# Perceiver layer on one core: heads stage reordered two groups ahead, and the row maxima of W1 taken in the cross-attention

## The chip, the cores and the metric

The kernel runs on one core of a Trainium2 chip (trn2). The metric is the device time of one execution in microseconds. Engines: PE is TensorE, DVE VectorE, ACT ScalarE, POOL GpSimd; SP issues most of the DMAs.

## The reference, cut to what matters

```python
def layer(x, ctx):                       # x [1, 256, 1024], ctx [1, 4096, 1024], all float32
    y = layernorm(x)                     # cross-attention
    Q, K = y @ Wq.T + bq, ctx @ Wk.T + bk
    x = x + softmax(Q @ K.T / sqrt(1024)) @ ctx
    y = layernorm(x)                     # latent attention, 128 heads, 8 content and 64 rope dims each
    cq, ckv = y @ Wq_down, y @ Wkv_down
    q_c, k_c, v_c = heads(cq @ Wq_up), heads(ckv @ Wk_up), heads(ckv @ Wv_up)
    q_r, k_r = heads(y @ Wq_rope), y @ Wk_rope          # k_r is shared by all heads
    s = (q_c @ k_c.T + q_r @ k_r.T) / sqrt(72)
    x = x + merge(softmax(s) @ v_c) @ Wo
    y = layernorm(x)                     # two quantized linears, 1024 -> 4096 -> 1024
    # linear8(x, W, b): columns of x whose maximum is over 3 stay whole; all else is rounded to
    # int8 codes, with a scale per row of x and a scale per row of W: max |W[n, :]| / 127
    return x + linear8(linear8(y, W1, b1), W2, b2)
```

## The kernel before, in words

Every product of float32 values is made of three float32r matmuls: each operand is split into a high part (a cast copy) and a low part (the value less its high part), and `product` (lines 45 to 51) issues high x high, high x low and low x high. ScalarE mostly makes the high parts, VectorE and GpSimd the low ones. Engines meet at semaphores, and each engine runs its own list in order. The stages follow each other in blocks, and an engine starts a block when all have ended the one before.

**Scores** (about 82 to 195 us). ctx comes in eight chunks of 512 rows, 2 MB each, into two `ring` buffers. TensorE turns a chunk while it multiplies the chunk before. Per chunk VectorE makes eight low parts, two score maxima, and the row maxima of two W2 panels: a panel is 128 rows x 1024 columns, 512 KB, loaded into `w2p` (`load_w2` L420, `maximum_w2` L425).

**Attend** (about 195 to 298 us). The chunks are loaded again. For each chunk ScalarE makes the exponentials, the high part of the chunk's rows (`high_rows`, L407) and the high part of the turned probabilities. VectorE and GpSimd make the low parts of two row tiles each (`low_rows`, L412), VectorE those of the probabilities (`low_p`, L675), and then VectorE takes two more W2 panels. TensorE works on chunk c while the parts of c + 1 are made. SP's list for a chunk: two panels, a wait for the low parts of the chunk (n_dve, n_pool), the load of the chunk after next. When all is done VectorE divides and adds for each of two row tiles (L701) and makes the layernorm.

**Projections** (302 to 329 us). Down and up projections; the content parts of q and k go to DRAM (`store_content`), in three slots of 128 rows, so that a group can read them back in another layout. VectorE copies the low and the high part of k_r to eight head slots each (L905, L906).

**Heads** (330 to 731 us). 128 heads in 32 groups of four. A group's rope weights (128 x 8 x 256, 1 MB) are loaded to `ring`, split by ScalarE (two `wh` copies, L774) and GpSimd (two subtractions, L780), and multiplied: `rope_q`, 48 matmuls, one PSUM bank for each pair of heads. ScalarE copies each head's q to `qrope` (L1117) and again to rows 0 to 63 of `qmix` (L1118); VectorE puts the low part on the other half of `qrope` (L1178). Rows 64 to 87 of `qmix`, `kmix_h` and `kmix_l` hold the content slots, read by GpSimd's three DMAs (L1232). `scores_q` (2 matmuls a head) gives rough scores from which VectorE takes negated maxima (L1187), `turn_max` turns them, ScalarE copies a row for each head to row 96 of `qmix` (L1143); `scores_k` (4 matmuls a head) gives key-major scores with the maximum subtracted; ScalarE makes exp (L1124) and its high part (L1128), VectorE the low part (L1183); `attend` (4 matmuls a head) multiplies with the values that GpSimd has put in place (L1240). VectorE also takes one W1 row tile's maxima per group (L1199). Per group TensorE has 48 + 8 + 2 + 16 + 16 = 90 matmuls. TensorE's order in a group is written out by hand in `step`: the scores of group g, the attend of g - 1 and the rope products of g + 1. In the last group ScalarE and VectorE also split three pairs of oT tiles (L947, L952) before the rest of their work.

After the heads come the output projection and the two linears (731 to 1061 us), which the change leaves as they are.

## Time and profile before

| | us |
|---|---|
| median of 3 runs | 1061.13 |
| lowest, highest | 1061.06, 1067.21 |
| profiled execution: span | 1060.9 |
| busy: PE, DVE, ACT, POOL | 962.6, 760.3, 697.2, 451.8 |

No time of the profiled execution is given apart from its span. A row of groups gives line, engine, operation, output <- inputs, count, then busy time, the mean of one in ns, and the idle time before with its releaser. Times in the timeline are us from the span's start. A matmul's duration in the profile is longer than its distance to the next, since they are pipelined.

### The profile page before, as it was taken

The page shows a single profiled execution, that of the slowest core. Times are in us where ns is not written, and L with a number is a line of the kernel's source. Part 1 is how long each engine was busy: PE and PEld are TensorE (multiplying, and loading weights), DVE is VectorE, ACT ScalarE, POOL GpSimd, SP SyncE. Part 2 cuts the span into 40 slices and gives each one's busy share as a digit, 9 for nine tenths or more (in the row PEclk, how much of TensorE's full clock was granted, in tenths as well). Part 3 has the DMA queues.
Part 4 walks back from the last instruction along what each step waited for, and adds up shares of the span by engine and source line. Part 5 has one row for each costly group of instructions (what it writes and reads, how often), then busy time and mean ns, then how long its engine had stood idle before and what let it go on. Part 6 is the DMA issues. An engine that isn't in the chain of part 4 may idle for free. (4 is left out here: it accounts for less than half of the span.)

```text
span 1060.9 us, 20413 instructions
## 1 busy us (share of the span) xinstructions
PE 962.6 (91%) x6771; PEld 881.5 (83%) x6771; DVE 760.3 (72%) x1212; ACT 697.2 (66%) x1270; POOL 451.8 (43%) x395
## 2 busy tenths in 40 slices
PE   6999999899978889999999999997859999599987
PEld 5998888688867888998999999986658999498986
DVE  6426566544474678888787889878797888798864
ACT  4424434545345788998999999995538777456562
POOL 0300000433335445655566556630147666355663
PEclk9999999999989899999999999996969999699999
DMA  7436665567625766455545554560424334223221
GB/s 278 160 120 219 237 212 202 215 254 274 201 89 159 204 201 200 156 172 152 154 141 166 175 152 142 174 226 1 159 79 153 111 134 158 80 80 144 95 80 40
DMA packets 71706, 168.36 MB, mean 159 GB/s; under 512 B 7504, under 2 KB 48496, under 8 KB 69104
## 3 DMA queue, kind: packets, MB, share of 16 engines
q1 hardware_dynamic: 66576, 158.35, 43.5%
q0 software_dynamic: 4608, 9.45, 3.6%
q8 instruction: 24, 0.39, 0.1%
q14 instruction: 18, 0.15, 0.0%
q10 hardware_dynamic: 480, 0.03, 0.0%
HBM read 160.46 MB, written 7.34 MB: 158 GB/s over the span
## 5 line engine op out<-in xcount | busy, mean ns | idle before, releaser
L780 POOL TENSOR_TENSOR wl<-ring,wh 128x1024 fp32r<-128x1024 f32 x64 | 153.5, 2400 | 109.8 <-ACT wh L774 109.8
L49 PE MATMUL bank<-act_all,W_all 128*128 128x256 f32 (+1 forms) x512 | 158.0, 309 | 10.7 <-POOL W_all L1483 7.9
L49 PE MATMUL bank<-act_all,wh 128*128 128x256 f32 x512 | 148.1, 289 | 2.0 <-PEq L785 2.0
L51 PE MATMUL bank<-act_all,W_all 128*128 128x256 f32 (+1 forms) x512 | 146.0, 285 | 0.0
L50 PE MATMUL bank<-act_all,wh 128*128 128x256 f32 x512 | 145.0, 283 | 0.0
L51 PE MATMUL bank<-act_all,wl 128*128 128x256 f32 x512 | 144.5, 282 | 0.0
L412 POOL TENSOR_TENSOR xa_WT_l<-ring,xa_WT_h 128x1024 fp32r<-128x1024 f32 x16 | 41.4, 2606 | 186.4 <-ACT xa_WT_h L407 186.4
L1483 POOL TENSOR_TENSOR W_all<-rnd,W_all 128x512 fp32r<-128x512 f32 x72 | 92.9, 1303 | 45.1 <-ACT W_all L1408 38.1
L49 PEld LDWEIGHTS bank<-act_all,W_all 128*128 128x128 f32 x512 | 99.8, 195 | 13.4 <-POOL W_all L1483 9.9
L1183 DVE TENSOR_TENSOR pl<-pexp,ph 128x512 fp32r<-128x512 f32 x128 | 85.8, 689 | 25.5 <-ACT ph L1128 25.1
L49 PEld LDWEIGHTS bank<-act_all,wh 128*128 128x128 f32 x512 | 98.9, 193 | 2.8 <-issue 2.8
L51 PEld LDWEIGHTS bank<-act_all,W_all 128*128 128x128 f32 x512 | 99.7, 195 | 0.0
L50 PEld LDWEIGHTS bank<-act_all,wh 128*128 128x128 f32 x512 | 98.4, 192 | 0.0
L51 PEld LDWEIGHTS bank<-act_all,wl 128*128 128x128 f32 x512 | 98.1, 192 | 0.0
L1785 POOL TENSOR_TENSOR W_all<-rnd,W_all 128x512 fp32r<-128x512 f32 x56 | 73.1, 1316 | 54.8 <-ACT W_all L1743 54.0
L1128 ACT ACTIVATE ph<-pexp 128x512 fp32r<-128x512 f32 x128 | 80.9, 632 | 10.6
L1178 DVE TENSOR_TENSOR qrope<-bank,qrope 64x256 fp32r<-64x256 f32 x128 | 54.0, 422 | 45.2 <-ACT qmix L1118 42.0
L1187 DVE TENSOR_REDUCE nmax<-bank 128x2 f32<-128x512 f32 x128 | 82.7, 688 | 3.6 <-PE bank L1017 2.5
L1035 PE MATMUL bank<-qrope,krope 128*128 128x256 f32 x256 | 71.9, 301 | 12.3 <-ACT qmix L1143 7.0
L774 ACT ACTIVATE wh<-ring 128x1024 fp32r<-128x1024 f32 x64 | 67.4, 1056 | 20.1 <-DMA ring<-in_L_attn_Wq_rope_dram 18.3
L1124 ACT ACTIVATE pexp<-bank 128x512 f32<-128x512 f32 x128 | 75.3, 588 | 2.7 <-PE bank L1036 1.2
L50 PE MATMUL bank<-W_all 128*128 128x256 f32 (+1 forms) x256 | 73.9, 289 | 0.0
(221 smaller groups left out, 2885.2 us busy)
## 6 DMA issues: line engine op xcount, KB each, us to landing
ring<-in_ctx_dram SPq DMA_DIRECT2D x16, 2048.0 KB, 8.7
ring<-in_L_attn_Wq_rope_dram SPq DMA_DIRECT2D x32, 1024.0 KB, 7.1
ring<-in_L_ffn_W_dram SPq DMA_DIRECT2D x16, 2048.0 KB, 7.5
w2p<-in_L_ffn_W_dram SPq DMA_DIRECT2D x32, 512.0 KB, 4.7
w1p<-in_L_ffn_W_dram SPq DMA_DIRECT2D x32, 512.0 KB, 3.5
ring<-in_L_xattn_Wq_dram SPq DMA_DIRECT2D x2, 2048.0 KB, 11.8
ring<-in_L_xattn_Wk_dram SPq DMA_DIRECT2D x2, 2048.0 KB, 7.9
ring<-in_L_attn_Wo_dram SPq DMA_DIRECT2D x2, 2048.0 KB, 11.4
```

Source lines behind the costliest of these rows:

```text
L49: pe.matmul(out, lh, rh, start=start, stop=False, skip_group_check=True)
L50: pe.matmul(out, lh, rl, start=False, stop=False, skip_group_check=True)
L51: return pe.matmul(out, ll, rh, start=False, stop=stop, skip_group_check=True)
L774: act.activation(wh[b][:, 4 * half:4 * half + 4, :], rope_raw(b)[:, 4 * half:4 * half + 4, :], ACT.Copy).then_inc(w_hi, 1)
L780: pool.tensor_tensor(wl[b][:, 4 * half:4 * half + 4, :], rope_raw(b)[:, 4 * half:4 * half + 4, :], f32(wh[b][:, 4 * half:4 * half + 4, :]) ...
L1035: pe.matmul(o, krope[:, kt * P:(kt + 1) * P], qrope[b][:, h, :], start=True, stop=False)
L1124: act.activation(pexp[h % 2][:, :, :].rearrange("p k q -> p (k q)"), bank[5 + h % 2][:, :], ACT.Exp, scale=RSQRT).then_inc(ex_ready, 1)
L1128: act.activation(ph[h][:, :, :], pexp[h % 2][:, :, :], ACT.Copy).then_inc(p_hi, 1)
L1183: dve.tensor_tensor(pl[h][:, :, :], pexp[h % 2][:, :, :], f32(ph[h][:, :, :]), ALU.subtract).then_inc(p_lo, 1)
L1187: dve.tensor_reduce(nmax[b][:, :, 32 * h:32 * h + 1], bank[3 + h % 2][:, :].rearrange("p (t k) -> p t k", t=QT), axis=AX.X, op=ALU.max, ne ...
L1483: pool.tensor_tensor(W_l[b][:, k, :], rnd[k % 4][:, :], f32(W_h[b][:, k, :]), ALU.subtract).then_inc(b_lo, 1)
L1785: pool.tensor_tensor(V_l[:, k, :], rnd[k % 4][:, :], f32(V_h[:, k, :]), ALU.subtract).then_inc(j_lo, 1)
```

## The change

**W1 maxima moved.** The panel buffers of scores and attend (now `panel`, still two) take W1 row tiles as well: per chunk of scores two W2 panels and one of W1, per chunk of attend two of W2 and three of W1; all 32 W1 tiles are done there, and the heads take none. SP loads panels 0 and 1 of a chunk ahead of the ctx load and the others behind it. A panel's load waits for the maximum taken from the panel two before it.

**Heads.** TensorE's step g now holds attend(g - 1), scores_k(g), scores_q(g + 1) and rope_q(g + 2), with three buffers for `qmix`, `qrope` and the key tiles. The loops are written out for all groups. ScalarE copies q once, to `qrope`; SP copies it from there to `qmix` by DMA (`duplicate`, two per pair of heads). `kmix` is the one key tile: it holds the low part of k_r (spread by three DMAs instead of sixteen casts), the same content rows for both kinds of scores, and in rows 96 to 99 a one for the own head; `krope` has two forms, one for heads with the high part of q in the lower half and one for the others. The four maxima rows are written by one operation (`max_rows`) to all four heads' rows 96 to 99. The second half of the weights' high part is copied by GpSimd instead of ScalarE. The content is read by SP, two DMAs per group instead of three by GpSimd, and the content stores come behind one another in the first six steps. The three oT copies of ScalarE stand at the start of the last step, VectorE's parts of them at its end.

```diff
-            w2_ready, w2_max = [sem("w2_ready0"), sem("w2_ready1")], sem("w2_max")
-            def load_w2(sp, n, j):
-                sp.wait_ge(w2_max, n * 2 + (j + 1))
-                sp.dma_start(w2p[j][:, :], w2_flat[:, ds(n * (2 * D) + j * D, D)]).then_inc(w2_ready[j], 16)
-            def maximum_w2(dve, n, j):
-                dve.wait_ge(w2_ready[j], n * 16 + 16)
-                dve.tensor_reduce(am2[:, ds(n * 2 + j, 1)], w2p[j][:, :], axis=AX.X, op=ALU.max,
-                                  apply_absolute_value=True).then_inc(w2_max, 1)
+            panel_ready, panel_max = [sem("panel_ready0"), sem("panel_ready1")], sem("panel_max")
+            IN_SCORES, IN_ATTEND = 3, 5
+            def load_panel(sp, q, b, src):
+                sp.wait_ge(panel_max, q + 1)
+                sp.dma_start(panel[b][:, :], src).then_inc(panel_ready[b], 16)
+            def maximum_panel(dve, b, uses, out):
+                dve.wait_ge(panel_ready[b], uses * 16 + 16)
+                dve.tensor_reduce(out, panel[b][:, :], axis=AX.X, op=ALU.max, apply_absolute_value=True).then_inc(panel_max, 1)
+            def w1_rows(n):
+                return w1_n[ds(n, 1)].rearrange("a p d -> p (a d)")
...
+            def attend_panels(i, b):
+                at = IN_ATTEND * b
+                return [(i * 10 + (NCTX * IN_SCORES + at + p), (at + p) % 2, i * 5 + (NCTX * IN_SCORES // 2 + (at + p) // 2))
+                        for p in range(IN_ATTEND)]
...
+                            load_panels(i, b, (0, 1))
                             sp.wait_ge(sb_ready, i * (2 * KT) + KT * (b + 1))
                             load(sp, b, raw(b), ctx_t[ds(i * 2 + (b + 2), 1)].rearrange("a p t d -> p (a t) d"))
+                            load_panels(i, b, (2,))
...
+                    def step(i, b, ahead):
+                        c = i * 2 + b
+                        panels = scores_panels(i, b)
+                        outs = (am2[:, ds(c * 2, 1)], am2[:, ds(c * 2 + 1, 1)], am1[:, ds(c, 1)])
                         for k in range(KT):
                             if ahead:
                                 low(1 - b, k, c * KT + (KT + k + 1))
-                            if k % 4 == 1:
-                                maximum_w2(dve, c, k // 4)
+                            if k in (1, 4, 6):
+                                p = (1, 4, 6).index(k)
...
+                        def load_panels(i, b, which):
+                            c = i * 2 + b
+                            sources = [w2_flat[:, ds(c * (2 * D) + (NCTX * 2 + j) * D, D)] for j in range(2)]
+                            sources += [w1_rows(c * 3 + (NCTX + j)) for j in range(3)]
+                            for p in which:
+                                q, buf, _ = attend_panels(i, b)[p]
+                                load_panel(sp, q, buf, sources[p])
                         with sp.Fori(0, NCTX // 2 - 1) as i:
                             for b in range(2):
-                                for j in range(2):
-                                    load_w2(sp, i * 2 + (NCTX + b), j)
+                                load_panels(i, b, (0, 1))
                                 sp.wait_ge(n_dve, i * 4 + 2 * (b + 1))
                                 sp.wait_ge(n_pool, i * 4 + 2 * (b + 1))
                                 load(sp, b, raw(b), ctx_t[ds(i * 2 + (b + 2), 1)].rearrange("a p t d -> p (a t) d"))
+                                load_panels(i, b, (2, 3, 4))
...
+                        def maxima(i, b):
+                            c = i * 2 + b
+                            outs = [am2[:, ds(c * 2 + (NCTX * 2 + j), 1)] for j in range(2)]
+                            outs += [am1[:, ds(c * 3 + (NCTX + j), 1)] for j in range(3)]
+                            for (_, buf, uses), o in zip(attend_panels(i, b), outs):
+                                maximum_panel(dve, buf, uses, o)
+                        def chunk(i, b):
+                            c = i * 2 + b
+                            low_rows(dve, c, b, (0, 1), n_dve)
+                            low_p(c, b)
+                            maxima(i, b)
...
+            QBUF = 3
             vals = sb(ml, "vals", [P, 2, QT, D], F32R)
-            krope = sb(ml, "krope", [P, T], F32R)
-            kmix_l = sb(ml, "kmix_l", [P, 2 * GROUP, T], F32R)
-            kmix_h = sb(ml, "kmix_h", [P, 2 * GROUP, T], F32R)
-            qmix = [sb(ml, f"qmix{i}", [P, GROUP, T], F32R) for i in range(2)]
+            krope = sb(ml, "krope", [P, 2, T], F32R)
+            kmix = sb(ml, "kmix", [P, QBUF * GROUP, T], F32R)
+            qmix = [sb(ml, f"qmix{i}", [P, GROUP, T], F32R) for i in range(QBUF)]
...
-            def split_w(act, b, half):
-                act.activation(wh[b][:, 4 * half:4 * half + 4, :], rope_raw(b)[:, 4 * half:4 * half + 4, :],
-                               ACT.Copy).then_inc(w_hi, 1)
-            def low_w(pool, g2, b):
-                for half in range(2):
-                    pool.wait_ge(w_hi, g2 * 2 + (half + 1))
-                    pool.tensor_tensor(wl[b][:, 4 * half:4 * half + 4, :], rope_raw(b)[:, 4 * half:4 * half + 4, :],
-                                       f32(wh[b][:, 4 * half:4 * half + 4, :]), ALU.subtract).then_inc(w_lo, 1)
+            def half_of(tile, half):
+                return tile[:, 4 * half:4 * half + 4, :]
+            def high_w(act, g):
+                landed(act, g % 2, USE_ROPE + g // 2)
+                act.activation(half_of(wh[g % 2], 0), half_of(rope_raw(g % 2), 0), ACT.Copy).then_inc(w_hi, 1)
+            def split_w(pool, g):
+                landed(pool, g % 2, USE_ROPE + g // 2)
+                h, l, r = wh[g % 2], wl[g % 2], rope_raw(g % 2)
+                pool.tensor_copy(half_of(h, 1), half_of(r, 1)).then_inc(w_hi2, 1)
+                pool.wait_ge(w_hi, g + 1)
+                pool.tensor_tensor(half_of(l, 0), half_of(r, 0), f32(half_of(h, 0)), ALU.subtract).then_inc(w_lo, 1)
+                pool.wait_ge(w_hi2, g + 1)
+                pool.tensor_tensor(half_of(l, 1), half_of(r, 1), f32(half_of(h, 1)), ALU.subtract).then_inc(w_lo, 1)
...
+                    sp.wait_ge(kr_hi, 2)
+                    for b in range(QBUF):
+                        sp.dma_start(f32(kmix[0:ROPE, b * GROUP:(b + 1) * GROUP, :]),
+                                     f32(krope[0:ROPE, 1, :]).unsqueeze(1).to_broadcast([ROPE, GROUP, T])).then_inc(k_spread, 16)
...
+                    def content(g):
+                        b = g % QBUF
+                        if g % 8 == 0:
+                            sp.wait_ge(stored[g // 8], 2 * SLOTS * 16)
+                        if g >= QBUF:
+                            sp.wait_ge(st_ready, (g - QBUF + 1) * GROUP)
+                        own = slice(b * GROUP, (b + 1) * GROUP)
+                        columns = slice((g % 4) * GROUP * T, (g % 4 + 1) * GROUP * T)
+                        for dst, i in ((qmix[b], 0), (kmix[:, own, :], 1)):
+                            src = content_dram[i][g // 4].rearrange("(r h) q -> r (h q)", h=HT)
+                            sp.dma_start(f32(dst[ROPE:ROPE + SLOTS * HEAD, :, :]).rearrange("p h q -> p (h q)"),
+                                         src[:, columns]).then_inc(mix_ready[b], 16)
+                    def duplicate(g, pair):
+                        b = g % QBUF
+                        sp.wait_ge(q_hi, g * GROUP + 2 * pair + 2)
+                        for s in range(2):
+                            h = 2 * pair + s
+                            sp.dma_start(f32(qmix[b][0:ROPE, h, :]),
+                                         f32(qrope[b][s * ROPE:(s + 1) * ROPE, h, :])).then_inc(dup_ready[b][pair], 16)
+                    def next_w(g):
+                        sp.wait_ge(w_lo, (g - 1) * 2)
+                        load(sp, g % 2, rope_raw(g % 2), rope_t[:, :, g * GC:(g + 1) * GC])
+                    next_w(2)
+                    for g in range(FIRST, NG):
+                        if valid(g + 2):
+                            content(g + 2)
+                            duplicate(g + 2, 0)
+                        if 0 <= g + 2 < 6:
+                            store_content(sp, 1 + (g + 2) // 2, (g + 2) % 2)
+                        if valid(g + 2):
+                            duplicate(g + 2, 1)
+                        if valid(g + 5):
+                            next_w(g + 5)
+                        elif g + 5 < NG + 2:
+                            b = (g + 5) % 2
+                            sp.wait_ge(w_lo, (g + 4) * 2)
+                            load(sp, b, raw(b), wo_t[:, CH * b:CH * b + CH, :])
...
+                    for g in range(FIRST, NG + 1):
+                        scores_q(g + 1, 0)
+                        attend(g - 1, 0)
+                        attend(g - 1, 1)
+                        rope_q(g + 2, 0, 0)
+                        scores_k(g, 0)
+                        rope_q(g + 2, 0, 2)
+                        attend(g - 1, 2)
+                        scores_q(g + 1, 1)
+                        rope_q(g + 2, 0, 4)
+                        attend(g - 1, 3)
+                        scores_k(g, 1)
+                        rope_q(g + 2, 0, 6)
+                        scores_q(g + 1, 2)
+                        scores_k(g, 2)
+                        rope_q(g + 2, 1, 0)
+                        scores_q(g + 1, 3)
+                        rope_q(g + 2, 1, 2)
+                        rope_q(g + 2, 1, 4)
+                        rope_q(g + 2, 1, 6)
+                        scores_k(g, 3)
+                        turn_max(g + 1)
 
...
+                    def max_rows(g):
+                        if not valid(g):
+                            return
+                        act.wait_ge(nt_ready, g + 1)
+                        act.activation(qmix[g % QBUF][96:100, :, :],
+                                       bank[2][0:GROUP, 0:T].unsqueeze(1).to_broadcast([GROUP, GROUP, T]), ACT.Copy).then_inc(m_row, 1)
...
+                    for g in range(FIRST, NG):
+                        next_w(g + 3)
                         if g == NG - 1:
                             for kk in range(KT // 2 - 1):
                                 act.wait_ge(o_norm, 4 * kk + 4)
                                 ot_high(act, kk)
-                        step(g, g % 2, USE_ROPE + 1 + g // 2, g < NG - 1, g < NG - 2)
+                        exps(g, 0)
+                        high_p(g, 0)
+                        exps(g, 1)
+                        high_q(g + 2, 0)
+                        high_p(g, 1)
+                        exps(g, 2)
+                        high_p(g, 2)
+                        high_q(g + 2, 1)
+                        max_rows(g + 1)
+                        exps(g, 3)
+                        high_p(g, 3)
...
+                    for g in range(FIRST, NG):
+                        maxima(g + 1, 0)
                         low_p(g, 0)
+                        maxima(g + 1, 1)
+                        low_q(g + 2, 0)
                         low_p(g, 1)
-                    low_q(0, 0, 0)
-                    step(0, 0, None, True, 1)
-                    with dve.Fori(0, NG // 4 - 1) as i:
-                        for j in range(4):
-                            step(i * 4 + (j + 1), (j + 1) % 2, (i * 4 + j, i, j), True, i * 2 + ((j + 1) // 2 + 1))
-                    for j in range(3):
-                        g = NG - 3 + j
+                        maxima(g + 1, 2)
+                        maxima(g + 1, 3)
+                        low_p(g, 2)
+                        if valid(g - 1):
+                            outputs(dve, g - 1)
+                            if (g - 1) % 4 == 3:
+                                divide(dve, (g - 1) // 4)
+                        low_q(g + 2, 1)
...
+                        values(g)
+                        if valid(g + 3):
+                            if g + 3 >= 2:
+                                pool.wait_ge(q_ready, (g + 2) * 2)
+                            split_w(pool, g + 3)
```

## Rows read from the trace of the kernel before

**Rows 1.** The page: busy time of each engine over the span.

```profile
PE 962.6 (91%) x6771; PEld 881.5 (83%) x6771; DVE 760.3 (72%) x1212; ACT 697.2 (66%) x1270; POOL 451.8 (43%) x395
```

**Rows 2.** Windows: length, busy us (count) of PE, PEld, DVE, ACT, POOL; PEclk; DMA share; GB/s.

```profile
125.00:150.00 25.00, 25.00 (x139) 20.73 (x138) 15.79 (x22) 9.66 (x18) 0.00 (x0) 1.00 0.62 220
226.66:238.73 12.07, 12.07 (x58) 9.83 (x57) 5.90 (x6) 6.27 (x10) 5.09 (x2) 1.00 0.68 258
329.90:731.00 401.10, 378.02 (x2880) 353.88 (x2880) 315.47 (x526) 349.78 (x705) 210.28 (x222) 0.97 0.55 166
422.33:705.22 282.89, 276.55 (x2162) 259.41 (x2161) 237.58 (x397) 262.65 (x529) 161.34 (x168) 1.00 0.52 161
694.41:705.22 10.81, 10.81 (x92) 10.64 (x91) 9.18 (x17) 10.31 (x22) 6.79 (x7) 1.00 0.63 231
```

**Rows 3.** Groups by line, 422 to 705 us: count, busy us, mean ns, idle before.

```profile
L780 POOL TENSOR_TENSOR wl<-ring,wh 128x1024 fp32r<-128x1024 f32 x48 | 115.4, 2405 | 75.5 <-ACT wh L774 75.5
...
L1183 DVE TENSOR_TENSOR pl<-pexp,ph 128x512 fp32r<-128x512 f32 x97 | 65.0, 689 | 18.5 <-ACT ph L1128 18.3
L1187 DVE TENSOR_REDUCE nmax<-bank 128x2 f32<-128x512 f32 x96 | 61.9, 688 | 0.9
L1128 ACT ACTIVATE ph<-pexp 128x512 fp32r<-128x512 f32 x97 | 61.4, 633 | 8.2
L1124 ACT ACTIVATE pexp<-bank 128x512 f32<-128x512 f32 x96 | 56.5, 589 | 1.2
...
L774 ACT ACTIVATE wh<-ring 128x1024 fp32r<-128x1024 f32 x48 | 50.7, 1056 | 5.5 <-DMA ring<-in_L_attn_Wq_rope_dram 4.9
...
L1178 DVE TENSOR_TENSOR qrope<-bank,qrope 64x256 fp32r<-64x256 f32 x96 | 40.5, 422 | 22.5 <-ACT qmix L1118 20.0
...
L1143 ACT ACTIVATE qmix<-bank 1x256 fp32r<-1x256 f32 x96 | 35.9, 374 | 2.4
L1117 ACT ACTIVATE qrope<-bank 64x256 fp32r<-64x256 f32 x96 | 35.9, 374 | 1.7
```

**Rows 4.** Timeline of SP in attend: start us, us, DMA issue.

```profile
201.28 1.50 SPq L423 DMA_DIRECT2D w2p<-in_L_ffn_W_dram  x2
...
235.06 0.33 SPq L121 DMA_DIRECT2D ring<-in_ctx_dram  x1
236.15 0.92 SPq L423 DMA_DIRECT2D w2p<-in_L_ffn_W_dram  x2
```

**Rows 5.** The page, DMA issues: KB each, median us from issue to landing.

```profile
ring<-in_L_attn_Wq_rope_dram SPq DMA_DIRECT2D x32, 1024.0 KB, 7.1
...
qmix<-content_q POOLq DMA_DIRECT2D x32, 96.0 KB, 2.5
```

**Rows 6.** Timeline of VectorE in attend, one chunk and the end.

```profile
227.75 2.36 DVE L412 TENSOR_TENSOR xa_WT_l<-ring,xa_WT_h 128x1024 fp32r<-128x1024 f32 x2 [5.21 <-ACT xa_WT_h L407]
...
232.28 2.33 DVE L427 TENSOR_REDUCE am<-w2p 128x1024 f32 x2
...
292.60 1.54 DVE L701 SCALAR_TENSOR_TENSOR xr<-bank,rden,xr 128x512 f32<-128x512 f32 x2 [9.51 <-PE bank L51]
...
298.19 1.54 DVE L701 SCALAR_TENSOR_TENSOR xr<-bank,rden,xr 128x512 f32<-128x512 f32 x2 [0.96 <-PE bank L51]
```

**Rows 7.** Landing of single DMAs issued near 196, 201, 235 and 236 us.

```profile
w2p<-in_L_ffn_W_dram SPq DMA_DIRECT2D x1, 512.0 KB, 3.6
...
w2p<-in_L_ffn_W_dram SPq DMA_DIRECT2D x1, 512.0 KB, 7.3
...
ring<-in_ctx_dram SPq DMA_DIRECT2D x1, 2048.0 KB, 7.9
w2p<-in_L_ffn_W_dram SPq DMA_DIRECT2D x1, 512.0 KB, 8.0
```

**Rows 8.** Windows: TensorE at a lower granted clock early in the heads.

```profile
358.40:365.20 6.80, 5.88 (x27) 5.88 (x28) 1.54 (x3) 6.36 (x14) 5.09 (x4) 0.50 0.96 303
```

**Rows 9.** Timeline of TensorE, the matmul before which it sat idle.

```profile
359.32 0.58 PE L1035 MATMUL bank<-qrope,krope 128*128 128x256 f32 x1 [2.96 <-ACT qmix L1143]
```

More of the change, by code:

```diff
@@ L194, in build @@
             rmax = sb(xs, "rmax", [P, QT])
-            w2p = [sb(xs, f"w2p{i}", [P, D]) for i in range(2)]
+            panel = [sb(xs, f"panel{i}", [P, D]) for i in range(2)]
             nbias = sb(xs, "nbias", [P, QT])
@@ L1034, in scores_k @@
                             o = bank[5 + h % 2][:, kt * T:(kt + 1) * T]
-                            pe.matmul(o, krope[:, kt * P:(kt + 1) * P], qrope[b][:, h, :], start=True, stop=False)
-                            last = pe.matmul(o, kmix_l[0:97, b * GROUP + h, kt * P:(kt + 1) * P], qmix[b][0:97, h, :],
-                                             start=False, stop=True)
+                            keys = slice(kt * P, (kt + 1) * P)
+                            pe.matmul(o, krope[:, h % 2, keys], qrope[b][:, h, :], start=True, stop=False)
@@ L1038, in scores_k, with attend @@
+                            last = pe.matmul(o, kmix[0:100, b * GROUP + h, keys], qmix[b][0:100, h, :], start=False, stop=True)
                         last.then_inc(st_ready, 1)
-                    def attend(g, b, h):
+                    def attend(g, h):
+                        if not valid(g):
+                            return
                         if h == 0:
                             pe.wait_ge(val_ready, g * 2 + 2)
-                            pe.wait_ge(o_done, g + 1)
-                        pe.wait_ge(p_lo, g * GROUP + (2 + h + 1))
+                            if g:
+                                pe.wait_ge(o_done, g)
+                        pe.wait_ge(p_lo, g * GROUP + h + 1)
@@ L1096, in _ @@
-                    pe.wait_ge(w_lo, 2)
-                    for pair in range(2):
-                        for k0 in range(0, KT, 2):
-                            rope_q(0, pair, k0)
-                    first_scores(0, 0, 1)
-                    step(0, 0, 1, None, True)
-                    with pe.Fori(0, NG // 2 - 1) as i:
-                        step(i * 2 + 1, 1, i + 2, i * 2, True)
-                        step(i * 2 + 2, 0, i + 2, i * 2 + 1, True)
-                    step(NG - 1, 1, None, NG - 2, False)
```

405 lines of the change are left out of this document (158 added, 247 removed).

## The prediction

> **What bounds the kernel now.** I read the page first: TensorE is busy for 91% of the span, so a gain must come from TensorE's idle time or its pace [rows 1]. Then I cut the span into stages [rows 2]. In a scores step and an attend step TensorE has no gap (25.00 of 25.00 us, 12.07 of 12.07). The heads stage takes 401.10 us for 2880 matmuls. Its 24 quiet groups take 282.89 us, 11.79 each, for 90 matmuls. The group between 694.41 and 705.22 takes only 10.81 us. That is the interval from which one of ScalarE's two weight copies is missing, because the last two groups split nothing. So the pace is ScalarE's. Its groups [rows 3] confirm it: per group of heads 4 x 0.633 (ph) + 4 x 0.589 (exp) + 2 x 1.056 (wh) + 12 x 0.374 (four qrope, four qmix, four maxima rows; L1117 costs what L1118 does) = 11.5 us in a period of 11.8. VectorE has 237.58 / 24 = 9.9 us of work per group [rows 2].
>
> **Heads: what goes.** ScalarE loses four qmix copies (1.5), four row copies (1.5) and one wh copy (1.06), and gains one operation for the four rows. Its 4x1024 elements from PSUM are not in the trace: below, one row copy, 0.37; above, the four it replaces, 1.5; I take 1.06, the 128x1024 copy, nearest in length. ScalarE: 11.5 - 4.1 + 1.1 = 8.5 us. VectorE loses the W1 maximum, 1.2: 8.7 us. GpSimd has two 2.4 us subtractions [rows 3] and now a copy of the same length, at most one more 2.4, and loses three DMA issues: 7.6 at most. SP issues seven DMAs per group at 0.3 to 0.5 each [rows 4], 3 us. None reaches the matmuls' 10.8, so TensorE becomes the bound. The matmul count is unchanged (100 instead of 97 rows of keys costs no column).
>
> Does the new order let it run? At 0.12 us a matmul, counted from a step's start: exp(g-1, 3) must end before scores_k(g, 1), matmul 42, 5.0 us. ScalarE does max_rows (to 1.1), exp and ph (to 2.3), wh (to 3.4); exp(g, 0) follows scores_k(g, 0). VectorE's fourth maximum of g+1 comes at about 9.8, and the transpose wants it at 10.6. Weights g+3 are split by about 8.3, wanted after 10.8. The tightest is q's second copy: rope_q(g+2) pair 0 ends at matmul 52, 6.2 us; two ScalarE copies 0.75, the second DMA issued at 7.6, landing in 2.5 as the 96 KB content read does [rows 5]: 10.1, wanted at 10.8. All fit, though two of them with some 0.7 us only.
>
> SP's new waits (ScalarE's qrope, then the end of the weights' split) hold the weights g+5 and the content g+3 behind them. Both are issued near a step's end and land some 7 us later, behind one another, and have more than a step [rows 5]. The content stores of the first six steps stand before the second pair's copy only, which is wanted 6 us into the next step. GpSimd no longer issues the content, so nothing of its queue waits for scores_k. For restarts after a wait I take 10.9 a step, bounds 10.8 (pure matmuls) and 11.8 (as before).
>
> The stage then: opening 17 us (rope_q(0) as before, 7; then scores_q(0) among rope_q(1), waiting for copies queued behind the second weights, 7.1 us [rows 5], and the first content), 30 steps x 10.9 = 327, and 16 for the two steps without rope_q and the last attend: 7.5 + 7 + 2, from VectorE's 4 x 0.688 + 4 x 0.689 + 1.2 in each [rows 3] and ScalarE's three oT copies. Together 360 us against 401: **-41 us** (-25 to -50). VectorE's wait for those oT copies in the last group before leaves with it.
>
> **Projections.** Fifteen VectorE casts go and three spreading DMAs come. TensorE ends that block at its own rate, so both count nothing; were the spread late, 1 or 2 us.
>
> **Scores.** Eight W1 maxima, one per chunk. VectorE is busy 15.79 of 25 us there and TensorE full [rows 2]; less than two maxima of 1.2 more per 25 us hide in the 9.2 left. The panel is queued behind the ctx load, which it meets well before k = 6. I take +0.5 (0 to 5): without cover it is 8 x 1.2 = 10.
>
> **Attend: the step that costs.** Five panels per chunk instead of two. In duration they fit: VectorE works 5.90 of 12.07 us [rows 2] and 3 x 1.2 more makes 9.5. But there are still two buffers, and SP issues: panels 0 and 1, the wait for the chunk's low parts, the ctx load of 2 MB, panels 2 to 4. Panel p waits for the maximum of p - 2. VectorE runs in order: low rows of chunk c, low_p, five maxima, and only then the low rows of c + 1. Before, its two panels had a chunk's time to land, even behind ctx. Now panel 2 is wanted in the chunk whose ctx load has just been queued before it. From the start of a chunk's low rows: low rows 2.4, to the issue of ctx 0.2, ctx lands 7.9 later, the panel behind it 1.2 after that (issued at 236.15 with 8.0 against 235.06 with 7.9), its maximum 1.2, issue 0.1, panel 4 lands in 3.6 (nothing ahead of it, as at 196), maximum 1.2 [rows 4, 6, 7]. Sum 17.8 us per chunk against 12.07. Panel 3 and its maximum lie inside that, low_p and maxima 0 and 1 beside ctx.
>
> Placed on the clock: panel 2 of chunk 0 is issued at 201.3 as the w2p of before and lands 7.3 later [rows 4, 7], 208.6; + 1.2 + 0.1 + 3.6 + 1.2 = 214.7, where chunk 1's low rows start. Five periods of 17.8 bring chunk 6 to 303.7; chunks 6 and 7 load 1 MB of rope weights (7.1 instead of 7.9), 17.0 each: chunk 7 starts at 320.7, its last maximum ends at 337.7. TensorE's last chunk is ready by then. VectorE next folds in both q tiles; the first took 292.60 to 297.2, the second began at 298.19 [rows 6]. Now the second begins at 337.7 + 0.3 + 4.6 = 342.6: **+44.4 us** (bounds 0, if the panels are there on time, and 58, if ctx and panel 4 each land 1 us later in seven chunks). The down weights, issued after panel 4, arrive at about the same time.
>
> On the granted clock: after TensorE had been idle for 2.96 us before 359.32, the window 358.40 to 365.20 shows 0.50, which is 1.2 GHz [rows 8, 9]. TensorE would idle 5.7 us per attend chunk. 6.8 us at half speed lose 3.4: 12.1 + 3.4 = 15.5, still under 17.8, so it costs nothing here. The Trainium skill, TensorE: Matmul & The Clock Gate, section HAM oscillation, says that a loop whose DMA waits open long gaps goes back to the slow clock in every turn. It speaks against the change; what it could cost is rival 3.
>
> **Sum.** 1060.9 (profiled span) + 44.4 + 0.5 - 41 = 1064.8, 1065 with the 0.2 us by which the median 1061.13 stands above the span. The time after the heads is shifted whole.
>
> **Rivals.** 1. Attend hides its panels, because loads of one queue overtake each other or ctx lands sooner. For it: VectorE's idle time and the 3.6 us of a lone panel; against: 8.0 us for a panel behind ctx. Then 1061 + 0.5 - 41 = 1021. It decides if the chain from low rows to the fifth maximum stays under 12.1.
> 2. Slower: the second copy of q lands late. If it takes more than about 3.2 us, TensorE waits at every scores_q(g, 0). Content queued with it was seen at 2.5, but on GpSimd's own queue; on SP's it stands behind the 1 MB weights, 7.1 us from issue near the step's start [rows 5], against a landing wanted at 10.8. A miss of 0.8 us makes 30 x 0.8 = 24: 1089. (The Trainium skill, DMA: Bandwidth & Descriptors, section Queues, rings and completion order: an engine alternates between queue rows but takes one row's ring in order. By it content loses its bypass; the sum stays while the weights land before 8 us.)
> 3. Slower: the slow clock holds throughout attend. A step of 24.1 instead of 17.8, seven times 6.3 = 44: 1109. Against: TensorE would work 12 of every 17.8 us, and the slow stretch of [rows 8] ended after 6.8 us with TensorE fed.
> 4. The change doesn't do what it says: ScalarE still sets the heads' pace. At 11.5 us a step the gain is 23 rather than 41: 1083. Against: 8.5 us of work.
>
> **Chances.** Forecast 0.56, rival 1 0.17, rival 2 0.17, rival 3 0.04, rival 4 0.06. The forecast's own range is 1050 to 1080, from heads -50 to -30 and attend +38 to +50. For 8 in 10 it must reach towards both sides: 1040 (half-hidden panels) to 1089 (late copies). Rival 1 stays outside. Under 1% nothing can be told from no change here. Faster (below 1050.5): rival 1 and the forecast's lower edge, 0.25. Within 1%: 0.46. Slower (above 1071.7): rivals 2 to 4 and the forecast's upper edge, 0.29.
>
> **What would show it.** Attend: VectorE waits for a DMA of panel in every chunk, some 6 us before the third and 2 before the fifth, and the low-row operations start 17.8 apart instead of 12.1. Heads: turn_max about 10.9 apart, ScalarE near 8.5 us per group, matmuls without gaps. I am wrong if the low rows of attend stay near 12 us apart, or if scores_q waits for a qmix DMA in each step of the heads.

## The result, and the profile after

The changed kernel takes 1123.2 us (median of 4 runs, 1120.1 to 1126.2) against 1061.1 for the kernel before: ratio 1.0577, 95% interval 1.0541 to 1.0612. The forecast was 1065 us, range 1040 to 1089. It is slower by 62 us where I expected 4. The profiled execution took 1126.17 us, with a span of 1124.4. The page of after, busy time of each engine, answers to [rows 1]:

```profile
PE 960.8 (85%) x6771; PEld 887.8 (79%) x6771; DVE 800.7 (71%) x1198; ACT 616.2 (55%) x1015; POOL 458.9 (41%) x331
```

ScalarE fell from 697 to 616 us, as the change intends. Yet the span grew. The windows of after, with the columns of [rows 2]: a scores step, the whole heads stage (first rope_q matmul to last attend matmul), and its 24 quiet groups:

```profile
125.00:150.00 25.00, 25.00 (x139) 20.73 (x138) 16.94 (x23) 9.91 (x17) 0.00 (x0) 1.00 0.68 263
379.43:795.90 416.47, 363.78 (x2880) 351.91 (x2880) 316.65 (x494) 268.95 (x450) 216.18 (x157) 0.96 0.48 133
441.66:748.25 306.59, 269.92 (x2163) 261.82 (x2161) 243.01 (x373) 201.44 (x337) 168.03 (x121) 0.98 0.44 121
```

Scores is as it was. The heads start at 379.43 instead of 329.90: +49.5. They last 416.5 us instead of 401.1: +15.4, where I had forecast -41. A quiet group takes 306.59 / 24 = 12.8 us, against 11.8 before and 10.9 in the forecast. TensorE has 12% of this window idle.

**Attend.** The timeline of VectorE in after, one chunk, answers to [rows 6]:

```profile
254.69 2.35 DVE L412 TENSOR_TENSOR xa_WT_l<-ring,xa_WT_h 128x1024 fp32r<-128x1024 f32 x2
256.96 1.28 DVE L708 TENSOR_TENSOR pt_l<-bank,pt_h 128x512 fp32r<-128x512 f32 x2
258.16 2.34 DVE L428 TENSOR_REDUCE am<-panel 128x1024 f32 x2
266.21 2.44 DVE L428 TENSOR_REDUCE am<-panel 128x1024 f32 x2 [5.71 <-DMA panel<-in_L_ffn_W_dram]
271.09 1.22 DVE L428 TENSOR_REDUCE am<-panel 128x1024 f32 x1 [2.44 <-DMA panel<-in_L_ffn_W_dram]
272.22 2.35 DVE L412 TENSOR_TENSOR xa_WT_l<-ring,xa_WT_h 128x1024 fp32r<-128x1024 f32 x2
...
346.13 1.54 DVE L740 SCALAR_TENSOR_TENSOR xr<-bank,rden,xr 128x512 f32<-128x512 f32 x2
```

This is what the forecast described: low rows 17.5 us apart, VectorE 5.7 us short of the third panel and 2.4 us short of the fifth. The second q tile's fold starts at 346.13 (forecast 342.6, before 298.19): +47.9.

**Heads.** Waits of TensorE (first line) between 441.66 and 748.25 us, then groups by line of the same stretch, as in [rows 3]:

```profile
PE bank L1142 <- issue: 32.1, 24, 2.2
```

```profile
L1259 DVE TENSOR_TENSOR pl<-pexp,ph 128x512 fp32r<-128x512 f32 x97 | 100.5, 1036 | 32.8 <-ACT ph L1215 31.7
L829 POOL TENSOR_TENSOR wl<-ring,wh 128x1024 fp32r<-128x1024 f32 x24 | 66.5, 2773 | 0.0
L1241 DVE TENSOR_REDUCE nmax<-bank 128x2 f32<-128x512 f32 x96 | 63.9, 687 | 1.5
...
L1193 ACT ACTIVATE qmix<-bank 4x1024 fp32r<-4x1024 f32 x24 | 24.3, 1011 | 0.6
```

Two things were not in the forecast. TensorE stands before L1142, the first attend matmul of a group, in all 24 groups, 32.1 us in total. And VectorE's low_p (L1259, L1183 before) takes 1036 ns on average instead of 689, with the same operands and size, while the maxima from PSUM (L1241) still take 687.

The profile names this wait "issue": it found no releaser for it. The timelines of after, around one such wait, show it: TensorE, VectorE, GpSimd.

```profile
568.62 0.48 PE L1098 MATMUL bank<-kmix,qmix 96*128 96x256 f32 x2
571.26 0.33 PE L1142 MATMUL bank<-ph,vgroup 128*96 128x256 f32 x1 [2.16 <-issue]
```

```profile
567.13 1.29 DVE L1241 TENSOR_REDUCE nmax<-bank 128x2 f32<-128x512 f32 x2
568.34 1.47 DVE L1259 TENSOR_TENSOR pl<-pexp,ph 128x512 fp32r<-128x512 f32 x1
569.84 0.42 DVE L988 COPY onat<-bank 32x256 f32<-32x256 f32 x1
570.29 0.42 DVE L989 COPY sx<-bank 32x256 f32<-32x256 f32 x1
570.75 0.41 DVE L991 TENSOR_TENSOR onat<-bank,onat 32x256 f32<-32x256 f32 x1
```

```profile
568.23 1.04 POOL L825 CAST wh<-ring 128x1024 fp32r<-128x1024 f32 x1 [3.09 <-PE bank L51]
```

L988 to L991 are `outputs`, which empties bank 7. The add ends at 571.16, and TensorE starts at 571.26: `attend(g, 0)` has `pe.wait_ge(o_done, g)`, because all groups accumulate into the one bank 7. That matmul stands 2 matmuls into TensorE's step, while VectorE runs `outputs` behind all four maxima and the third low_p. The same lines show the second cost: low_p starts at 568.34 while GpSimd's copy runs (568.23 to 569.27) and ends at 569.81, 0.54 us behind the end of that copy.

The granted clock falls as well: behind four of the six gaps of 2.15 us in the quiet groups (469.57, 571.26, 622.88 and 674.50 us), behind none of the gaps of 1.1 us there. Window of after:

```profile
571.90:575.30 3.40, 3.40 (x19) 3.40 (x18) 1.55 (x3) 0.78 (x2) 2.97 (x2) 0.51 1.00 291
```

0.51 is 1.2 GHz, so these 3.4 us lose 1.7. Steps (from one `turn_max` to the next) last 11.95 us, and 13.2 or 14.5 around VectorE's division (L997, 1.75 us, every fourth group), which makes the wait longest. In [rows 8, 9] such a fall of the clock behind a gap was seen once in the kernel before.

### The profile page after: what moved, and what is told of

Same layout as the page of the kernel before. It is cut to its first block and busy times, and to the rows that moved or that the text cites. A ratio compares the mean times of both kernels' runs of the same rounds, so it can differ in the third digit from the quotient of the medians.

```text
span 1124.4 us, 19077 instructions
## 1 busy us (share of the span) xinstructions
PE 960.8 (85%) x6771; PEld 887.8 (79%) x6771; DVE 800.7 (71%) x1198; ACT 616.2 (55%) x1015; POOL 458.9 (41%) x331
## 5 line engine op out<-in xcount | busy, mean ns | idle before, releaser
L49 PE MATMUL bank<-act_all,W_all 128*128 128x256 f32 (+1 forms) x512 | 157.3, 307 | 11.1 <-POOL W_all L1522 8.1
L1259 DVE TENSOR_TENSOR pl<-pexp,ph 128x512 fp32r<-128x512 f32 x128 | 127.2, 994 | 47.5 <-ACT ph L1215 46.2
L428 DVE TENSOR_REDUCE am<-panel 128x1024 f32 (+1 forms) x64 | 76.9, 1213 | 66.1 <-DMA panel<-in_L_ffn_W_dram 66.1
L827 POOL TENSOR_TENSOR wl<-ring,wh 128x1024 fp32r<-128x1024 f32 x32 | 78.5, 2452 | 85.2 <-ACT wh L819 85.1
L1142 PE MATMUL bank<-ph,vgroup 128*96 128x256 f32 x256 | 71.0, 302 | 46.3 <-issue 42.2
L49 PEld LDWEIGHTS bank<-act_all,W_all 128*128 128x128 f32 x512 | 99.2, 194 | 13.4 <-POOL W_all L1522 10.2
L1241 DVE TENSOR_REDUCE nmax<-bank 128x2 f32<-128x512 f32 x128 | 85.2, 687 | 5.7 <-PE bank L1098 3.8
L829 POOL TENSOR_TENSOR wl<-ring,wh 128x1024 fp32r<-128x1024 f32 x32 | 87.9, 2747 | 0.0
L1142 PEld LDWEIGHTS bank<-ph,vgroup 128*96 128x96 f32 x256 | 44.2, 173 | 53.2 <-issue 47.9
```

Of the source, the lines that this page charges most:

```text
L49: pe.matmul(out, lh, rh, start=start, stop=False, skip_group_check=True)
L428: dve.tensor_reduce(out, panel[b][:, :], axis=AX.X, op=ALU.max, apply_absolute_value=True).then_inc(panel_max, 1)
L827: pool.tensor_tensor(half_of(l, 0), half_of(r, 0), f32(half_of(h, 0)), ALU.subtract).then_inc(w_lo, 1)
L829: pool.tensor_tensor(half_of(l, 1), half_of(r, 1), f32(half_of(h, 1)), ALU.subtract).then_inc(w_lo, 1)
L1142: last = pe.matmul(bank[7][0:VCOLS, 0:T], vgroup[g % 2][:, kt, h * VCOLS:(h + 1) * VCOLS], part[h][:, kt, :], start=(h == 0 and kt == 0 an ...
L1241: dve.tensor_reduce(nmax[g % 2][:, :, h:h + 1], bank[3 + h % 2][:, :].rearrange("p (t k) -> p t k", t=QT), axis=AX.X, op=ALU.max, negate=T ...
```

## The experiments

**First round: each suspect alone, and the two of the heads together.**

`outputs_early`, bank 7 emptied earlier in VectorE's list:

```
                         maxima(g + 1, 1)
+                        if valid(g - 1):
+                            outputs(dve, g - 1)
                         low_q(g + 2, 0)
...
                         low_p(g, 2)
-                        if valid(g - 1):
-                            outputs(dve, g - 1)
-                            if (g - 1) % 4 == 3:
-                                divide(dve, (g - 1) // 4)
+                        if valid(g - 1) and (g - 1) % 4 == 3:
+                            divide(dve, (g - 1) // 4)
```

> Theory A, bank 7's single turn: TensorE stands before attend(g-1, 0) because VectorE copies bank 7 out only near the end of its list. With outputs(g-1) taken right behind maxima(g+1, 1), nothing else changed, that wait goes: heads steps from 11.95 / 13.2 / 14.5 (mean 12.5) to about 11.2, 30 of them, 40 us less, 1083 us; the idle time ahead of the attend matmuls falls from 46 us to under 5. Theory B, VectorE's slow low_p beside GpSimd sets the pace whatever the order: the wait only moves to another place, steps stay near 12.3, above 1110 us.

Measured: 1093.2 us, 30 less. Steps 11.65 and 12.06 (with division). TensorE's wait at the attend matmuls is gone (0.6 us left between 441 and 748); a smaller one at `turn_max` has come. Theory A holds for about three quarters of its size. Waits of TensorE in that stretch, and the timelines of GpSimd (first) and VectorE around one low_p:

```profile
PE bank L1110 <- DVE nmax L1241: 23.1, 25, 1.2
PE bank L1142 <- DVE pl L1259: 0.6, 1, 0.6
```

```profile
570.44 2.39 POOL L827 TENSOR_TENSOR wl<-ring,wh 128x1024 fp32r<-128x1024 f32 x1 [3.94 <-ACT wh L819]
```

```profile
571.54 1.84 DVE L1259 TENSOR_TENSOR pl<-pexp,ph 128x512 fp32r<-128x512 f32 x1 [0.68 <-ACT ph L1215]
573.30 0.68 DVE L1241 TENSOR_REDUCE nmax<-bank 128x2 f32<-128x512 f32 x1
```

GpSimd's L827 ends at 572.83 and low_p at 573.38, 0.55 behind it.

`pool_short`, GpSimd with little to do:

```
-pool.tensor_tensor(half_of(l, 0), half_of(r, 0), f32(half_of(h, 0)), ALU.subtract)
+pool.tensor_tensor(half_of(l, 0)[:, :, 0:8], half_of(r, 0)[:, :, 0:8], f32(half_of(h, 0)[:, :, 0:8]), ALU.subtract)
(and the same for half 1; wl cleared once before)
```

> GpSimd subtracts only 8 of the 256 columns of each half of the rope weights, so the low part of the weights is left out of q's rope product; its two subtractions of 2.4 us per group become about 0.2. Theory B, contention: low_p (0.99 us mean, 0.69 alone) falls back to about 0.70 for most of its 128, VectorE finishes its list some 1.0 us earlier per group and the outputs come earlier, so steps fall by about 1 us: 30 us less, 1093. Theory A alone (only the order counts, the slow low_p hang on something else than GpSimd): low_p stays at 0.99 and the time within 1% of 1123.

Measured: 1102.5 us, 20.7 less. Group of low_p over the whole span:

```profile
L1260 DVE TENSOR_TENSOR pl<-pexp,ph 128x512 fp32r<-128x512 f32 x128 | 88.2, 689 | 42.8 <-ACT ph L1216 41.6
```

All 128 are back at 689 ns without any edit to VectorE's program. GpSimd is the cause of the slow ones. TensorE still waits for bank 7 (28.2 us between 430 and 740), so A and B are separate. Every full step but the first now takes 11.9 to 12.0 us, those with the division too, and the granted clock is 1.00 from 389 to 758 us. In after the ordinary steps took 11.95 already: as long as bank 7's turn sets the pace, the slow low_p costs nothing there, and the 21 us come from the steps around the division and from the clock.

`both_heads` is the two edits together.

> Both edits to the heads together: outputs(g-1) early, and GpSimd's low part of the weights left out. If the two causes are all that keeps the heads from the forecast 10.9 us a step, steps are 10.8 to 11.0 and the time is 1123 - 30 x 1.6 = 1075 us; if a third cause exists (late copies of q, ScalarE), steps stay above 11.5 and the time above 1090.

Measured: 1071.0 us, 52.2 less than the changed kernel, against 30.0 + 20.7 = 50.7 for the two alone. Window of the heads stage:

```profile
377.60:740.00 362.40, 348.46 (x2880) 340.51 (x2880) 289.08 (x493) 266.11 (x450) 69.60 (x158) 1.00 0.55 153
```

362.4 us: the forecast had 360 for this stage. Most ordinary steps take 10.62, those with the division 11.35, and the granted clock is 1.00. In the forecast's parts: the opening takes 15.3 us (forecast 17), the 30 full steps 327.2 (327), the end 19.9 (16). There is no third cause of any size: the order's arithmetic was right once these two are out of the way. GpSimd was not quite out of the way: 18 low_p still met its copy, and their mean over the run was 790 ns.

`attend_two`, attend without its W1 panels:

```
-IN_SCORES, IN_ATTEND = 3, 5
+IN_SCORES, IN_ATTEND = 3, 2
(am1[:, 8:32] set to a constant; load_panels(i, b, (2, 3, 4)) and the three maxima left out)
```

> Attend without its 24 W1 panels and their maxima (left out of the result), two W2 panels per chunk as in the kernel before. Forecast step on record: the panels behind the ctx load cost 44.4 us. So 1123 - 48 = 1075 us, low rows 12.1 us apart, heads as long as they were. Rival: attend is slower for another reason (contention with GpSimd's low rows, the slow clock); then part of the 17.8 us period stays, and the time is over 1085.

Measured: 1077.9 us, 45.3 less; the heads start at 332.8. Timeline of VectorE, two chunks:

```profile
218.02 2.36 DVE L412 TENSOR_TENSOR xa_WT_l<-ring,xa_WT_h 128x1024 fp32r<-128x1024 f32 x2 [6.27 <-ACT xa_WT_h L407]
230.11 2.36 DVE L412 TENSOR_TENSOR xa_WT_l<-ring,xa_WT_h 128x1024 fp32r<-128x1024 f32 x2 [5.22 <-ACT xa_WT_h L407]
```

12.09 us apart, and from the first low rows to the second fold it is 96.3 us, as in before (96.0). So the panels are the whole of attend's loss. The heads start 2.9 us later than in before; 1.8 of that is there when attend begins (VectorE's first `pt_l` at 200.50 instead of 198.70; 198.85 in after).

`ctx_last` asks what about the panels costs the time: SyncE issues the five panels of a chunk first and the ctx load behind them.

```
-load_panels(i, b, (0, 1))
+load_panels(i, b, (0, 1, 2, 3, 4))
 sp.wait_ge(n_dve, ...); sp.wait_ge(n_pool, ...); load(sp, b, raw(b), ctx_t[...])
-load_panels(i, b, (2, 3, 4))
```

> The changed kernel with only SyncE's order in attend's loop changed: the chunk's five panels first, the ctx load of 2 MB behind them. Theory of the forecast (queue order and two buffers set attend's period): panel 2 no longer stands behind 2 MB, the chain becomes low rows 2.4 + low_p 1.4 + maximum 1.2 + panel 3.6 + maximum 1.2 + panel 3.6 + maximum 1.2 = 14.6 us instead of 17.8, if ctx has the next chunk to land in: six chunks x 3.2 = 19 us less, 1104. Rival: the bytes set it (4.5 MB per chunk), then the period stays near 17.8, within 5 us of 1123; or ctx is now late for ScalarE's high rows, then over 1123.

Measured: 1113.9 us, 9.3 less: half of what I expected. Timeline of VectorE:

```profile
262.03 2.35 DVE L412 TENSOR_TENSOR xa_WT_l<-ring,xa_WT_h 128x1024 fp32r<-128x1024 f32 x2
264.30 1.28 DVE L707 TENSOR_TENSOR pt_l<-bank,pt_h 128x512 fp32r<-128x512 f32 x2
267.38 2.42 DVE L428 TENSOR_REDUCE am<-panel 128x1024 f32 x2 [1.79 <-DMA panel<-in_L_ffn_W_dram]
272.49 1.22 DVE L428 TENSOR_REDUCE am<-panel 128x1024 f32 x1 [2.70 <-DMA panel<-in_L_ffn_W_dram]
274.84 1.22 DVE L428 TENSOR_REDUCE am<-panel 128x1024 f32 x1 [1.14 <-DMA panel<-in_L_ffn_W_dram]
277.48 1.22 DVE L428 TENSOR_REDUCE am<-panel 128x1024 f32 x1 [1.41 <-DMA panel<-in_L_ffn_W_dram]
278.61 2.35 DVE L412 TENSOR_TENSOR xa_WT_l<-ring,xa_WT_h 128x1024 fp32r<-128x1024 f32 x2
```

The 5.7 us wait behind 2 MB is gone, so the queue's order did set it. But the period is 16.6, not 14.6: the next chunk's first two panels now queue behind ctx (1.79), and each further panel is waited for by itself. Whether the bytes alone would allow 12.1 was not tried. Five panels and ctx are 4.72 million bytes per chunk, 391 GB/s at 12.07 us. The highest rate over a stretch of that length in `ctx_last`, with the DMA engines busy throughout:

```profile
292.00:304.07 12.07, 9.38 (x39) 7.36 (x38) 7.94 (x8) 4.79 (x6) 1.76 (x1) 0.86 1.01 385
```

At 385 GB/s the bytes of a chunk take 12.3 us (an estimate). So rival 1, a chain under 12.1, had next to no room in any order of the loads, but the 4 us between 12.3 and 16.6 are the order's and the two buffers', and no run here tried to get them.

**Second round: what a long GpSimd instruction costs, and where the W1 maxima should stand.** All of these have the early outputs and do all of the work.

`quarters`:

```
-pool.tensor_tensor(half_of(l, 0), half_of(r, 0), f32(half_of(h, 0)), ALU.subtract).then_inc(w_lo, 1)
+for k in range(0, 4):
+    pool.tensor_tensor(l[:, k, :], r[:, k, :], f32(h[:, k, :]), ALU.subtract).then_inc(w_lo, 1)
(half 1 likewise; the waits on w_lo count 8 per group)
```

> The outputs-early kernel, with GpSimd's two subtractions of 128x1024 per group cut into eight of 128x256 (same data, same work). Theory B1, VectorE's two-operand low_p waits until the GpSimd instruction that is running has ended (in outputs_early one took 1.84 us and ended 0.56 us behind GpSimd's L827): pieces of some 0.6 us let it wait 0.6 us at most, its mean falls from 0.98 to 0.85 or less, the waits ahead of turn_max (19.7 us in 21 between 450 and 700) go, steps fall from 11.6 to about 11.0: 1073 to 1080 us. Theory B2, the two engines share bandwidth while they overlap: mean of low_p stays at 0.98 or more and the time at 1090 or more.

Measured: 1083.0 us, 10.2 less than `outputs_early`; steps 11.03 and 12.18. The mean of low_p fell only from 980 to 935 ns, less than B1 wanted: the worst are 1.3 us instead of 2.2, but more of them meet a piece. The time lies between the two expectations; that it fell at all, with the same bytes moved, speaks for waiting and against sharing.

`w1_heads` takes the 24 W1 panels from attend to steps 5 to 28 of the heads:

```
+                        if 5 <= g < 29:
+                            dve.wait_ge(w1_in[(g - 1) % 2], ((g - 1) // 2 - 1) * 16)
+                            dve.tensor_reduce(am1[:, NCTX + g - 5:NCTX + g - 4], w1p[(g - 1) % 2], axis=AX.X, op=ALU.max,
+                                              apply_absolute_value=True).then_inc(w1_max, 1)
(behind low_p(g, 3); SyncE issues the panel one step earlier, after store_content)
```

> The outputs-early kernel with attend's 24 W1 panels and maxima taken from attend to the heads, one each in steps 5 to 28, last in VectorE's list (two buffers in the half of the second staging buffer that is free then). All of the work is done. Forecast step on record: attend gives back 45 us as in attend_two: 1093 - 45 = 1048 us if the maxima of 1.2 us hide in VectorE's idle time. Rival: VectorE is the path in the heads (it is late for turn_max), then each costs its 1.2 us: 24 x 1.2 = 29, 1077 us.

Measured: 1057.0 us, 36.2 less than `outputs_early`: attend's 45 back, 9 lost elsewhere. The maxima do not cost these 9 us: the steps that hold one take 11.65 and 12.06, as in `outputs_early`. They hide, as the theory said. TensorE loses the time near the end of the heads:

```profile
705.55 0.76 PE L1105 MATMUL bank<-kmix,qmix 96*128 96x256 f32 x2 [3.83 <-DMA kmix<-content_k]
```

SyncE stands in the new wait for the last W1 maximum (`w1_max`, 24), which ends at 695.06; only then does it issue a load of 2 MB and, behind it at 696.04, the content of the last group. The granted clock is 0.50 from 705.5 to 709, another 1.7 us. A wait of 2.6 to 3.3 us for the same load stands in each of the kernels below; no run removed it. The rest is 2.8 us ahead of the first full step and 2.8 us behind the heads. The opening differs by as much between kernels whose openings are alike (14.5 to 18.0 us); the cause of either stays open.

`w1_heads_quarters`:

> w1_heads and quarters together, all work done. If the waits for GpSimd's instructions were what made VectorE late (B1), the W1 maxima find room: 1048 - 15 = about 1033 us, steps 10.9 to 11.2. If B2 holds or the list is too long anyway (8.4 us of VectorE work + 1.2 in 10.9), over 1048.

Measured: 1056.4 us, no gain from the pieces here; steps went from 11.04 to 11.73 when the W1 maxima began. VectorE's timeline showed why:

```profile
521.83 0.87 DVE L1261 TENSOR_TENSOR qrope<-bank,qrope 64x256 fp32r<-64x256 f32 x2
524.01 0.69 DVE L1268 TENSOR_TENSOR pl<-pexp,ph 128x512 fp32r<-128x512 f32 x1 [1.31 <-ACT ph L1224]
524.62 1.21 DVE L1287 TENSOR_REDUCE am<-ring 128x1 f32<-128x1024 f32 x1
525.87 0.69 DVE L1250 TENSOR_REDUCE nmax<-bank 128x2 f32<-128x512 f32 x1
```

VectorE stands 1.31 us before low_p(g, 3), and the W1 maximum comes directly behind it.

`w1_heads_quarters_act`:

> As w1_heads_quarters, with GpSimd's high copy of half of the rope weights (1.04 us per group) on ScalarE instead. ScalarE has 8.5 + 1.06 = 9.6 us of work in a step of 10.9. If ScalarE's order has room, the last waits of low_p (those on L825's copy) go and the time is that of w1_heads_quarters or up to 10 us below it; if ScalarE is late with high_p or high_q, 5 to 20 us above it.

Measured: 1061.9 us, 5.5 above: GpSimd's copy on ScalarE is a loss, though low_p fell from 866 to 784 ns. The wait before `turn_max` stayed.

`w1_mid_quarters` and `w1_mid_whole` put the maximum one place earlier:

```
                         low_q(g + 2, 1)
+                        (the W1 maximum)
                         low_p(g, 3)
-                        (the W1 maximum)
```

> w1_heads_quarters with the W1 maximum one place earlier in VectorE's list: between low_q(g+2, 1) and low_p(g, 3), where VectorE stands 1.31 us for ScalarE's ph in each step, instead of behind low_p(g, 3), where it pushed maxima and low_p(g+1, 0) back by 1.2 us. Theory: the maximum then costs nothing, TensorE's wait of 1.3 us before turn_max goes in most steps, steps fall from 11.7 to 10.9 in three of four (the fourth has the division): about 20 us less, 1035 us. Rival: the position is indifferent, because the sum of VectorE's work is the path: within 5 us of 1056.

> The same order with GpSimd's subtractions whole instead of in eight pieces (w1_heads with the W1 maximum one place earlier). If waiting for a whole GpSimd instruction costs VectorE some 0.8 us per step beyond waiting for a piece, 10 to 25 us above w1_mid_quarters (as 1093 against 1083 for outputs_early and quarters); if VectorE's idle time takes it up, within 3 us of it.

Measured: 1046.5 us with the pieces (ratio to the kernel before 0.9858, 0.9839 to 0.9877), 1066.6 with whole subtractions. Ordinary steps take 11.03 again, so the maximum has become free; the steps with the division take 13.19, VectorE's 1.75 + 0.43 more, where they had taken 12.16. That is why only 9.9 of the expected 20 us came. The 20.1 us between the two versions are as expected. The timeline of VectorE in `w1_mid_whole` shows what whole subtractions do to this order:

```profile
507.88 1.93 DVE L1266 TENSOR_TENSOR pl<-pexp,ph 128x512 fp32r<-128x512 f32 x1
509.83 0.69 DVE L1248 TENSOR_REDUCE nmax<-bank 128x2 f32<-128x512 f32 x1
510.44 2.14 DVE L1266 TENSOR_TENSOR pl<-pexp,ph 128x512 fp32r<-128x512 f32 x1
```

low_p averages 1031 ns there and 874 in `w1_heads`. The W1 maximum has one operand and passes beside GpSimd: in `w1_heads` 38 of the 64 panel maxima overlap a GpSimd instruction and take 1.21 to 1.22 us, as the 26 others do. My reading, argued and not tested: behind low_p(g, 3) it filled the time in which the next low_p would have waited (the first low_p of a group averages 1399 ns in `w1_heads`, 1794 in `w1_mid_whole`).

`w1_mid_sums_act`, one copy of `outputs` on ScalarE, as its text says:

> w1_mid_quarters with one of VectorE's three operations of outputs (the copy of bank 7's sums, 0.42 us) on ScalarE, behind exps(g, 1). In w1_mid_quarters VectorE has 10.6 us of work in a step of 11.03 and its idle time is almost gone, so VectorE's sum is the path: theory, 0.4 us less in each of 24 to 30 steps, 10 to 13 us less, about 1035 us, steps of 10.6 and 12.8. Rival: TensorE's 90 matmuls (10.6) and its waits for p_lo set the pace already, then within 4 us of 1046; or ScalarE's 0.37 us more ahead of high_q makes q's second copy late, then over 1050.

Measured: 1043.8 us (0.9839, 0.9814 to 0.9865), 2.6 less, within the rival's 4 us and not the 10 to 13 of the theory. The steps with the division fell from 13.19 to 12.74, by the 0.42 moved and no more; ordinary steps stayed at 11.05. Waits of VectorE between 400 and 680 us:

```profile
DVE qrope L1272 <- ACT qrope L1200: 8.8, 19, 0.5
DVE pl L1279 <- ACT ph L1229: 4.8, 18, 0.3
```

The first of these waits is new (before the move, VectorE's only one of any size was 7.3 us for `ph`): VectorE waits for ScalarE instead. What holds the ordinary steps at 11.05, where `both_heads` had 10.62, was not taken apart. This version is 18 us faster than the kernel before and 79 faster than the change.

## Why the prediction was wrong

- **Attend, +44.4: right.** Measured +47.9 in the trace and 45.3 by taking the panels out. Queue order, two buffers and the two waits per chunk were as stated. The 3.5 us beyond the forecast are about the size of one stall: at 232.76 two low rows took 6.67 us instead of 2.35 beside GpSimd's low rows (see below). In `pool_short`, whose attend is the same, no low rows stalled, and the second fold starts at 342.54, forecast 342.6.
- **Scores, +0.5: right.** TensorE has no gap in the window, and attend begins 0.15 us later than before.
- **Heads, -41: wrong, +15.4 measured.** The failed step is "Does the new order let it run?", the list of deadlines, with its verdict "All fit" and 10.9 a step: the 30 full steps took 376.0 us, 12.5 each. It left out the wait of `attend(g, 0)` for `o_done`. By the forecast's own numbers it does not fit: VectorE's fourth maximum at 9.8, low_p 0.69, outputs 1.3 give 11.8, wanted at 10.9 + 0.24 = 11.1. `outputs_early` puts this omission at 30 us.
- **The second failed term is low_p at 0.689**, taken from rows in which VectorE hardly ever met GpSimd. In the new order it does, at more than every third low_p: 1036 ns in the quiet groups. `pool_short` puts this at 21 us. VectorE's 8.7 us of work a step became 10.1 (243.01 / 24), and the 1.4 are these four low_p. Both together give 52, and the stage lands at 362.4 of the forecast 360.
- **ScalarE at 8.5 us a step: right** (201.44 / 24 = 8.4, the new row operation 1.01 for 1.06). ScalarE idles, so rival 4 is out. **Rival 2 is out too**: q's second copy lands 2.0 us after issue by the page, where 3.2 was the limit. **Rival 3** (the slow clock throughout attend) is out: the low rows start 17.0 to 18.4 us apart, once 21.9, and not 24.1. But the clock did fall in part. Its mean in attend went from 0.98 (before, 196 to 298 us) to 0.86 (196 to 346), which added nothing to the waits: in `pool_short` it was 0.85, and attend took what was forecast. And it fell in the heads, behind gaps that no rival had.
- The range failed with the heads: its upper end, 1089, allowed one late copy, not two causes of 20 and 30 us.

```profile
qmix<-qrope SPq DMA_DIRECT2D x128, 64.0 KB, 2.0
```

## What to carry to other kernels

When an order written by hand is rearranged, list every semaphore wait of the engine that is to become the bound and put a time on each from both sides; the one for a reused accumulator is easily missed, since its releaser is a small operation far down another engine's list. A duration read from the old order holds only for operations that meet the same company in the new one: two-operand SBUF work on VectorE and any work on GpSimd should be laid out as if they were one engine. Where VectorE waits anyway is the place for filler such as weight maxima, and a queue's big load belongs behind the small ones that are wanted in the same turn. A wait put into a queue's list holds back every load behind it, also those that have nothing to do with it.

## What the runs showed of the hardware

VectorE's subtraction of two SBUF operands and GpSimd's instructions exclude each other. In after, of the low_p between 400 and 760 us that stand alone in their row, 41 began while a GpSimd instruction was running, with more than 0.2 us of it to go. Every one of them ended 0.54 to 0.56 us after that instruction's end, whatever its start; their mean is 1.64 us. The 29 that were running when GpSimd's began took 0.68, as the 45 without company did, and then GpSimd's instruction is the longer one (a subtraction takes 2.70 or 2.85 us instead of 2.39). VectorE's maxima, with one operand, were not slowed (0.69 us from PSUM, 1.21 from SBUF). The Trainium skill, SBUF — State Buffer, section SBUF: two separate sides, states this rule, an exclusive lock held for a whole instruction; the trace agrees, and I had not weighed it. In the profile such a wait is no idle time: it stands in the instruction's own duration, so only the mean ns of a group gives it away. In attend it can cost more. VectorE and GpSimd in after:

```profile
232.76 6.67 DVE L412 TENSOR_TENSOR xa_WT_l<-ring,xa_WT_h 128x1024 fp32r<-128x1024 f32 x2
```

```profile
232.71 5.64 POOL L412 TENSOR_TENSOR xa_WT_l<-ring,xa_WT_h 128x1024 fp32r<-128x1024 f32 x2 [8.73 <-ACT xa_WT_h L407]
```

Both began their two low rows together, GpSimd 0.05 us first, and VectorE came away 4.3 us late; TensorE stood 10.3 us at its next wait for VectorE's `pt_l`.
